# The last attention by query tiles, and the last sequence's end in two halves of tokens

## What is computed

```
scores = q @ k.T / 4 + bias[b, head] (512 x 512, float32), masked keys get -1e30
src    = norm(...) + softmax(scores) @ v @ Wo + bo
out    = src + gelu2((norm(src) * g2 + beta2) @ W1 + b1) @ W2 + b2
```

## Time and profile before

| | before |
|---|---|
| median of 3 runs | 1198.31 us (1197.61 to 1201.12) |
| the profiled execution | 1193.41 us |
| its span, first to last instruction | 1191.5 us |
| PE busy | 987.8 us (83%) |
| PEld, DVE, ACT, POOL busy | 55%, 62%, 58%, 38% |
| mean granted clock of TensorE | 0.961 |

### The profile page before, as it was taken

One profiled execution on the slowest core, in us unless ns is written; L12 is line 12 of the kernel. 1 busy time (PEld: TensorE's weight loads), 2 busy tenths in 40 slices (PEclk: granted clock), 3 DMA queues, 4 the chain that ended last, 5 costly groups with the idle time before them and its releaser, 6 DMA issues.

```text
span 1191.5 us, 22171 instructions
## 1 busy us (share of the span) xinstructions
PE 987.8 (83%) x7620; PEld 653.0 (55%) x7620; DVE 735.1 (62%) x1965; ACT 691.7 (58%) x1603; POOL 447.7 (38%) x672
## 2 busy tenths in 40 slices
PE   5377889898898797888789898799789998689768
PEld 2144555556465365555555576456466575447545
DVE  4368774564837638866773557746874857564750
ACT  1256666473746554676556556675666667366732
POOL 8000020000100636646035003945779436685820
PEclk9589999999899998999999999999899999899989
DMA  7846512405012564575623227557483456944700
GB/s 207 217 122 183 101 37 74 105 1 142 1 37 63 142 160 145 165 196 172 160 86 95 60 89 172 181 161 200 149 217 126 137 170 182 238 146 132 240 1 18
DMA packets 118113, 155.83 MB, mean 131 GB/s; under 512 B 12716, under 2 KB 80684, under 8 KB 118004
## 3 DMA queue, kind: packets, MB, share of 16 engines
q1 hardware_dynamic: 111748, 146.26, 44.5%
q10 hardware_dynamic: 4256, 4.19, 1.4%
q0 software_dynamic: 2000, 3.97, 1.3%
HBM read 135.51 MB, written 18.88 MB: 130 GB/s over the span
## 4 chain that ended last, share of the span: by engine, by line
PE 44%; DVE 20%; ACT 11%; issue 9%; DMA 8%; POOL 5%; SPq 2%; ACTq 0%; DVEq 0%; POOLq 0%
PE bank L1241 14%; PE bank L1230 7%; PE bank L1315 6%; PE bank L1329 4%; POOL bias L739 4%; PE bank L1297 4%; DVE bias L1086 3%; DVE mrow L1080 3%; DMA bias<-in_fside_Bx16xSxS 3%; PE bank L1196 3%; DMA k_parts<-gT 2%; ACT gT L816 2%; SPq L573 2%; DMA ks<-k_parts 2%; ACT bias L768 2%
## 5 line engine op out<-in xcount | busy, mean ns | idle before, releaser
L739 POOL TENSOR_TENSOR bias<-bias,negmask 128x256 f32<-128x256 f32 x512 | 334.5, 684 | 277.3 <-DMA bias<-in_fside_Bx16xSxS 271.5
L768 ACT ACTIVATE bias<-bias,mrow 128x512 f32<-128x512 f32 x256 | 184.2, 720 | 204.2 <-DVE mrow L1086 202.9
L1086 DVE CUSTOM_DVE_ANT_0 bias<-bank,bias 128x512 f32<-128x512 f32 x256 | 175.1, 687 | 189.5 <-PE bank L1297 167.8
L765 ACT ACTIVATE prob<-bank,mrow 128x128 f32<-128x128 f32 (+3 forms) x256 | 135.0, 528 | 198.2 <-DVE mrow L1080 196.8
L1297 PE MATMUL bank<-ks,qs 128*128 128x512 bf16 (+3 forms) x512 | 179.5, 351 | 69.1 <-ACT prob L765 35.5
L1080 DVE TENSOR_REDUCE mrow<-bank 128x1 f32<-128x128 f32 (+3 forms) x256 | 124.4, 487 | 174.6 <-PE bank L1300 173.4
L1315 PE MATMUL bank<-ident,bias 128*128 128x128 f32 x1024 | 161.2, 281 | 55.8 <-ACT pT L776 44.4
L1230 PE MATMUL bank<-hT,w 128*128 128x512 f32 x384 | 184.1, 610 | 11.0 <-ACT gT L816 9.9
L1315 PEld LDWEIGHTS bank<-ident,bias 128*128 128x128 f32 x1024 | 123.2, 144 | 122.7 <-ACT bias L768 70.9
L1241 PE MATMUL bank<-w,gT 128*128 128x256 f32 x768 | 174.3, 381 | 0.0
L1241 PEld LDWEIGHTS bank<-w,gT 128*128 128x128 f32 x768 | 142.5, 190 | 20.2 <-issue 2.7
(11 more groups left out here) (152 smaller groups left out, 1129.8 us busy)
## 6 DMA issues: line engine op xcount, KB each, us to landing
bias<-in_fside_Bx16xSxS SPq DMA_DIRECT2D x128, 512.0 KB, 4.6
w<-in_L_cond_W SPq DMA_DIRECT2D x16, 1024.0 KB, 5.5
qs<-q_parts SPq DMA_DIRECT2D x30, 384.0 KB, 9.7
ks<-k_parts SPq DMA_DIRECT2D x30, 384.0 KB, 11.4
q_parts<-gT SPq DMA_DIRECT2D x80, 128.0 KB
k_parts<-gT SPq DMA_DIRECT2D x48, 128.0 KB
w<-in_L_cond_Wi SPq DMA_DIRECT2D x4, 1024.0 KB, 5.1
w<-in_L_cond_Wo SPq DMA_DIRECT2D x4, 1024.0 KB, 5.5
```

Of the source, the lines that this page charges most:

```text
L739: pool.tensor_tensor(b_n, b_n, negmask[:, t, keys], ALU.add).then_inc(masked, 1)
L765: act.activation(prob_of(U), score_bank[U % 2][:, 0:n], ACT.Exp, bias=mrow[:, U % ROW_RING:U % ROW_RING + 1], accum_out=rsum[:, U % ROW_RI ...
L768: act.activation(prob_of(U), prob_of(U), ACT.Exp, scale=-1.0, bias=mrow[:, U % ROW_RING:U % ROW_RING + 1], accum_out=rsum[:, U % ROW_RING: ...
L1086: v.tensor_tensor_reduce(out=prob_of(U), in0=score_bank[U % 2][:], in1=prob_of(U), scale=-1.0, scalar=3e38, op0=ALU.add, op1=ALU.min, accu ...
```

## The change

In the last attention the query tile is outermost (`unit`): units 448 to 463 are tile 0 with all heads, and so on; a batch is one tile, `values` and `normalize` write accordingly. The second half of the heads is first read in unit 456 and not in 480, and its stack moves from tick 452 to 449. The end of sequence 3 becomes two halves of 256 tokens, each planned by `plan_half`: the first from tick 488, when two tiles are normalized, the second from tick 520. Each half projects, adds, normalizes, turns, does the eight hidden steps and gelus on its 256 columns, its two `ff_out` into bank 1, its addition, and a store from SP's queue. A half does its own two `bn_aggr`; the small rsqrt steps run in full in both. The gelu groups come in ticks 499, 503 and 506. The copies of units 486 to 494 go to ACT by the planner's costs and those of units 495 to 506 to DVE, where before they alternated. POOL's mask terms come in ticks 444, 460, 476 and 492 instead of 444, 452, 460 and 468. ACT's final wait for the stores becomes SP's.

```
+def plan_half(t, s, i):
+    at(t, "pe", "project", s, 1, i)
+    at(t + 1, "v", "residual", s, 1, i)
+    at(t + 2, "v", "stats", s, 6, i)
+    for r in range(RSQRT_STEPS):
+        at(t + 3 + r // SLOTS, f"v{r % SLOTS}", "rsqrt", s, 6, r, i)
+    at(t + 6, "v", "apply", s, 6, i)
+    at(t + 7, "p", "res_l3_half", s, i)
+    at(t + 7, "pe", "turn_half", s, i)
+    at(t + 8, "v", "feature_cols", s, i)
+    at(t + 8, "a", "feature_cols", s, i)
+    t += 10
+    for j, (dt, da) in enumerate(zip((0, 0, 1, 3, 4, 5, 7, 8), (1, 1, 1, 5, 5, 5, 8, 8))):
+        at(t + dt, "pe", "hidden_cols", s, i, j)
+        at(t + da, "a", "gelu_cols", s, i, j)
+    for x in range(2):
+        at(t + 9 + x, "pe", "ff_out", s, 2, 2 * i + x)
+    at(t + 11, "v", "ff_add", s, 2, i)
+    at(t + 12, "sp", "store_half", s, i)
...
-STACKS_AT = [(-6, 5)] + [(-28, 4)] * 2 + [(-7, 4)] + [(-28, 4)] * 3 + [(-7, 4)]
+STACKS_AT = [(-6, 5)] + [(-28, 4)] * 2 + [(-7, 4)] + [(-28, 4)] * 3 + [(-7, 1)]
...
-    [(9, norm(6), 3), (15, block3, 3)],
...
+HALF_AT = [40, 72]
+for _i, _t in enumerate(HALF_AT):
+    plan_half(UNITS * LAST_ATT + _t, LAST_SEQ, _i)
...
             c, t, e, j = u // (2 * NT * GH), u // (2 * GH) % NT, u // GH % 2, u % GH
+            if a == LAST_ATT:
+                t, c = u // (4 * GH), u // (2 * GH) % 2
...
+            def store_half(s, i):
+                sp.wait_ge(ff_done, 2 * FFN[s, 2] + i + 1)
+                tt = slice(2 * i, 2 * i + 2)
+                sp.dma_start(out[s].rearrange("(t p) d -> p t d", p=P)[:, tt, :], xy[s][:, tt, :]).then_inc(stored, 16)
...
+            def res_l3_half(s, i):
+                pool.wait_ge(tok[5], NT * NTH[s, 5] + 2 * (i + 1))
+                for t in (2 * i, 2 * i + 1):
+                    res(pool.tensor_tensor(xy[s][:, t, :], xy[s][:, t, :], b2[1][:], ALU.add))
...
+            def gelu_cols(s, i, j):
+                n, cols = FFN[s, 2], slice(HALF * i, HALF * (i + 1))
+                act.wait_ge(f1_psum, NF * (n + i) + j + 1)
+                act.activation(gT[:, j, cols], dense_bank[FF_BANK[j]][:, cols], ACT.Gelu_apprx_sigmoid,
+                               bias=b1[2][:, j:j + 1]).then_inc(g_done, 1)
...
+            def turn_half(s, i):
+                dense_banks_free(issued)
+                pe.wait_ge(ff_done, 2 * FFN[s, 2] + i)
+                for t in (2 * i, 2 * i + 1):
+                    pe.wait_ge(tok[5], NT * NTH[s, 5] + t + 1)
+                    for c in range(ND):
+                        mm = pe.transpose(dense_bank[c][:, t * P:(t + 1) * P], h[:, t, c * P:(c + 1) * P], ident[:])
...
+            def hidden_cols(s, i, j):
...
+                if j >= 3:
+                    pe.wait_ge(g_done, NF * (n + i) + j - 2)
+                for c in range(ND):
+                    mm = pe.matmul(dense_bank[FF_BANK[j]][:, cols], w1[:, c, j * P:(j + 1) * P], hT[:, c, cols],
+                                   start=c == 0, stop=c == ND - 1)
...
             def project(s, l, i):
-                if i == 0:
+                if ATT[s, l] == LAST_ATT:
+                    dense_banks_free(issued)
+                    pe.wait_ge(ff_done, 2 * FFN[s, 2] + i)
+                    pe.wait_ge(ctx_norm, BATCHES * LAST_ATT + 2 * (i + 1))
+                elif i == 0:
...
             def scores(U):
-                if U % (UNITS // 2) == 0:
+                if a == LAST_ATT and U % UNITS in (0, 2 * GH) or a != LAST_ATT and U % (UNITS // 2) == 0:
                     pe.wait_ge(stack_in[hd // HH], 96 * (a + 1))
```

More of the change, by code:

```diff
@@ L243, in plan_loads @@
 def plan_loads():
-    ffns = sorted((first_tick("pe", "hidden", s, f), s, f) for s in range(B) for f in range(3))
+    ffns = sorted((first_tick("pe", "hidden_cols" if (s, f) == (LAST_SEQ, 2) else "hidden", *((s,) if (s, f) == (LAST_SEQ, 2) else (s, f))), s, f)
+                  for s in range(B) for f in range(3))
     for n, (_, s, f) in enumerate(ffns):
@@ L286 @@
 TURN = order("pe", "turn_tokens", lambda a: a)
+TURN[LAST_SEQ, 5] = len(TURN)
 NTH = {(s, k): sum(1 for x in TURN if x[1] == k and TURN[x] < n) for (s, k), n in TURN.items()}
+NTH[LAST_SEQ, 5] = sum(1 for x in TURN if x[1] == 5) - 1
 FFN = order("pe", "hidden", lambda a: a[:2])
+FFN[LAST_SEQ, 2] = len(FFN)
 QKV = order("pe", "qk", lambda a: a[:2])
@@ L293 @@
               for t0, sf in sorted((t, a[:2]) for t, e, st, a in EVENTS if e == "pe" and st == "hidden" and a[2] == 0)}
+QKV_BEFORE[LAST_SEQ, 2] = len(ATTENTIONS)
 ADAPT = order("pe", "down", lambda a: a[0])
 assert QKV == ATT and OUTP == ATT and all(ADAPT[s] == s for s in range(B))
[L298 removed]
+V_LOAD = {"stats": 8, "rsqrt": 2, "apply": 9, "apply_late": 9, "feature_half": 7, "feature_cols": 4, "rest": 8, "lo": 8, "v": 8, "residual": 14,
           "ff_add": 12, "expert": 3, "up_add": 7}
[L300 removed]
+A_LOAD = {"feature_half": 7, "feature_cols": 4, "hi": 7, "mid": 7, "gelu": 10, "gelu_cols": 8, "down": 20, "expert": 6}
 def copy_sides():
@@ L502, in res_count @@
                                            if e == "p" and st.startswith("res")):
-                total += NT * (2 if step == "res_l0" else 1)
+                total += {"res_l0": 2 * NT, "res_l3_half": NT // 2}.get(step, NT)
                 if step == name and args[0] == s:
+                    return total
+                if step == "res_l3_half" and (s, layer) == (LAST_SEQ, 3) and args[1] == i_half:
                     return total
@@ L613, in _ @@
                     do[step](*args)
+            sp.wait_ge(stored, 16 * (B + 1))
         @block.gpsimd
@@ L793, in feature_half, with feature_cols @@
                                    bias=norm_w[w][:, 2:3]).then_inc(hT_a, 1)
+            def feature_cols(s, i):
+                cols = slice(HALF * i, HALF * (i + 1))
+                act.wait_ge(t_psum, TURN[s, 5] + 1 + i)
+                act.activation(hT[:, 0, cols], dense_bank[0][:, cols], ACT.Identity, scale=norm_w[2][:, 0:1],
+                               bias=norm_w[2][:, 2:3]).then_inc(hT_a, 1)
             def hi(s, l, i):
@@ L939, in _, with rsqrt @@
             chain = [0]
-            def rsqrt(s, k, i):
+            def rsqrt(s, k, i, half=None):
                 var, bits, guess, sq = nwt[:, 0, :], nwt[:, 1, :], rstd[:], nwt[:, 2, :]
@@ L946, in rsqrt @@
                 if i == 0:
-                    for t in range(NT):
+                    tiles = range(NT) if half is None else range(2 * half, 2 * half + 2)
+                    for t in tiles:
                         count[0] += 1
                         ins = v.bn_aggr(mv[:, t, :], stats[:, t, :])
-                        if t < NT - 1:
+                        if t < tiles[-1]:
                             ins.then_inc(vec, 1)
@@ L1218, in project @@
                 mm.then_inc(wo_psum, 1)
-                if i == 1:
+                if i == 1 and ATT[s, l] != LAST_ATT:
                     issued["out"] += 1
@@ L1237, in ff_out @@
                     pe.wait_ge(w2_in, 16 * (n + 1))
+                done = NF * (n + 1) if (s, f) == (LAST_SEQ, 2) and t == 2 else NF * n
                 for j in range(NF):
-                    if t == 0 and j in (0, 6, 7):
-                        pe.wait_ge(g_done, NF * n + max(6, j + 1))
-                    mm = pe.matmul(dense_bank[FF_OUT_BANK[t // 2]][:, (t % 2) * D:(t % 2 + 1) * D],
+                    if (t == 0 or done > NF * n) and j in (0, 6, 7):
+                        pe.wait_ge(g_done, done + max(6, j + 1))
+                    mm = pe.matmul(dense_bank[ff_out_bank(s, f, t // 2)][:, (t % 2) * D:(t % 2 + 1) * D],
                                    gT[:, j, t * P:(t + 1) * P], w2[:, j, :], start=j == 0, stop=j == NF - 1)
@@ L1244, in ff_out @@
                     mm.then_inc(f2_psum, 1)
-                if t == NT - 1:
+                if t == NT - 1 and (s, f) != (LAST_SEQ, 2):
                     issued["ffn"] += 1
```

49 lines of the change are left out of this document (36 added, 13 removed).

## The result

The changed kernel took 1210.01 us (median of 5 runs, 1201.68 to 1210.66) where the kernel before took 1198.31: ratio 1.0072, with a 95% interval of 1.0044 to 1.0100. It is slower; the forecast was 1199.7 with 1191 to 1206, so the result lies outside the range. The ratio and its interval are estimated from all the runs; the plain quotient of the two medians is 1.0098, so the size of the loss is known only as some 0.4 to 1.0%.

A forecast was written before the change was run, and what follows sets the result against it. Bounds: GpSimd's bias masks in the last attention's second half, then a serial 46.0 us tail. Terms 4.8 + 2.3 + 12.9 - 18.6 = +1.4 us on 1193.41 gave 1194.8, as median 1199.7; range 1191 to 1206.

The forecast's parts named there:

- Part 4: Start of the last attention: unit 456 waits for stack 1, landing at 1041, delaying sequence 2's block; cost 4.8 us.
- The reordered bias addresses I cost at nothing: Start of the last attention: reordered bias loads hidden under PE's work up to 1098 or behind the last load; cost nothing.
- If a bias load were late, POOL would pass it on one for one: Start of the last attention: any lateness of a bias load passes through POOL in full; no size given.
- 16.2 after the landing: From stack 1's landing to the turn of sequence 2's block: 4.8, 10.3 and 1.1 us, so the turn begins at 1057.2.
- Part 3: Ticks 488 to 497: POOL is the limit and gets a mask tile of 1.77 us more; cost 2.3 us (1.8 to 5).
- The rival "by VectorE in ticks 488 to 497": Ticks 488 to 497: cost 5 and a late first turn, +4 us in all, 1203.7 us; chance 0.06.
- Part 2: Ticks 498 to 509: half block beside the attention, ScalarE the limit, 28.2 us for 15.1; cost 12.9 us (10.7 to 14.7).
- The rival by the tables: Half block's gelus: each of six table switches holds ScalarE 1.38 us longer than its row, 1208 us; chance 0.02.
- Part 1: Tail after the last ctxn: half the tokens take 27.4 us instead of 46.0; saved 18.6 us (16.8 to 20.2).
- +1.4: Whole kernel: net of the four parts, 4.8 + 2.3 + 12.9 - 18.6 us, giving 1199.7 us.
- The rival "by the late stack": Start of the last attention: unit 456 waits for stack 1 until 1046.4, +5.4 us over the forecast, 1205.1 us; chance 0.22.

The follow-up runs named there:

- experiment 8: Kernel before with only stack 1's loads moved from tick 452 to 449, its order of units kept: 1206.34 us, ratio 1.0048.
- experiment 2: Changed kernel with units ordered by pairs of query tiles, stack 1 first read in unit 464, its loads still in tick 449: 1207.69 us, ratio 1.0092.
- 5: Changed kernel with units ordered by pairs of query tiles and stack 1 back in tick 452: 1201.64 us, ratio 1.0003.
- 4: Changed kernel by pairs of tiles, stack 1 in tick 449, first half's hidden and output layers moved behind the attention, from tick 521: 1198.59 us, ratio 1.0002.
- 6: Changed kernel by pairs of tiles, first half's hidden and output layers behind the attention, stack 1 in tick 452: 1195.47 us, ratio 0.9959.
- experiment 1: Kernel before with only the last attention's query tile outermost and stack 1 in tick 449, the end left whole: 1209.23 us, ratio 1.0108.
- experiment 9: Changed kernel with POOL's mask added to only 2 of each 256 columns for units 456 to 463 and 488 to 503: 1206.54 us, ratio 1.0064.
- experiment 7: As 6, but the first half's projection, addition, norm and turn start in tick 506 instead of 488: 1191.91 us, ratio 0.9922.
- experiment 3: Changed kernel with the first half's eight gelus replaced by copies with a bias, so without their table loads: 1206.41 us, ratio 1.0075.
- experiment 10: Changed kernel with POOL's mask additions in pieces of 512 columns instead of 256: 1220.84 us, ratio 1.0194.

## Why the prediction was wrong

**Part 4, the start (4.8 forecast, 10.7 measured), is the step that failed.** Its first half was right: the landing of stack 1 came within 0.2 us of 1041. Two things were wrong behind it.
- "The reordered bias addresses I cost at nothing: they lie under PE's work up to 1098 or behind the last load." Two bias loads had been put behind six loads of the stack, and I wrote only that they left the stack's path, not that they now stand in its shadow. Alone this costs 4.2 us in the trace (experiment 8), and undoing it gave 4.1 us back from experiment 2 to 5 and 6.7 from 4 to 6. "If a bias load were late, POOL would pass it on one for one" was the right mechanism and stood there without a price.
- "16.2 after the landing" took 21.9. By its three terms: from the landing to unit 457's maximum 5.8 (4.8 forecast), from there to the end of the rsqrt 14.2 (10.3), the first tile and the turn 1.9 (1.1). Most of the error is the middle term. I let VectorE's norm chain run at its speed of before, 0.16 us a step with POOL idle, and struck out the 2.95 us wait for POOL. But POOL's additions, late with their bias load, now ran beside it: one step took 2.96 and three took 0.6. With the mask loads on SP's queue the middle term was 11.5, but the first 6.8; the stage gave 2.4 us back. How much of the remainder is the reader of unit 456 alone I did not separate: order by tiles with the stack in tick 452 was not run.

**Part 3, ticks 488 to 497 (2.3 forecast, 5.5 measured).** I took POOL for the limit, since it was 12.88 us busy in 13.4, and priced what POOL got. The mask term costs at most 0.2 (experiment 1), so POOL had slack there for nearly all of its 1.8. What costs is what I took for covered: PE's projection, 2.0 us behind the scores of unit 488 with all later transposes and scores queued behind it, and VectorE's chain beside POOL. Taking POOL's additions away gave 2.7 of the 5.5 back (experiment 9), and taking the first half's work away gave all of it (experiment 7). How the 5.5 divides between PE's projection and VectorE's chain was not separated further. The rival "by VectorE in ticks 488 to 497", with 0.06, named the second of the two and put this stage at 5.

**Part 2, ticks 498 to 509 (12.9 forecast, 12.8 measured), was right**, and for its reason. The nine hidden ticks took 18.5 us (18.8 forecast) and the two output ticks 9.4 (9.4). Without the table loads (experiment 3) the nine took 15.1, near the 15.9 of PE's work alone, and ticks 502 and 506, in which PE turns units 500 and 504, were each 1.7 shorter; the forecast had waits of 1.3 and 1.6. So PE's own work is the larger part of the cost, and the wait for ScalarE the rest. As in the earlier trace rows, the gelu begins 0.02 us after its table load. The Trainium skill (ScalarE: Activation LUTs, What ACT_TABLE_LOAD costs) adds a drain of 1.38 us to each switch; the trace does not agree, there is no room for it between 1138.57, 1139.87 and 1141.09. The rival by the tables falls.

**Part 1, the tail (saved 18.6 forecast, 17.3 measured).** The projection is 2.1 us and not 1.1: the row of 1.98 was already that of one half, eight passes. The aggregates to the first hidden matmul took 5.0 for 4.6. Half clock came again (0.50 granted from 1177.3 to 1184.1, behind a stretch in which PE idled), and the hidden layer took 9.0, with 8.7 forecast. The store took 2.6 for 3.1.

**The sum.** 5.9 from part 4, 3.2 from part 3 and 1.3 from part 1 make 10.4 on top of +1.4: 11.8. The medians differ by 11.7; that the two agree so closely is luck, for the ratio of 1.0072 makes 8.6 us of it, and the traces of the two kernels differ by 8.1. The rival "by the late stack" had the place (the start) but not the cause: the stack landed when forecast. The trade was a poor one even as forecast: most of the 17.3 us of tail went into 12.8 us in ticks where PE and ScalarE had work of their own, and the start took more than the rest. What pays is a hole: experiments 4, 6 and 7 put the same matmuls where PE idled anyway.

## What to carry to other kernels

When a transfer is moved up in a queue, price both sides: what it delays behind it is a term of the sum, with the reader of each delayed load named. An engine at 96% busy is not the limit if it runs ahead of its readers; look at who waits for it. And small operations of VectorE must be priced at the speed that they have beside a busy GpSimd, from rows in which both work.

## What the runs showed of the hardware

- **VectorE beside GpSimd.** A 128x4 operation of a norm chain took 0.15 to 0.17 us with POOL idle. Beside POOL's additions of 0.65 us some still took that, but many took 0.5 to 0.7, and beside additions of 1.14 us (experiment 10) up to 1.07 in the chain shown. The Trainium skill (SBUF — State Buffer, Who interferes with whom) says that the two share one pair of ports as an exclusive lock, held for a whole instruction; the trace agrees, in that the wait grew with POOL's instruction.
- **A load issued by GpSimd can hold a VectorE operation for 2.9 us.** In the traces of the kernel before, of the changed kernel and of experiments 7 and 9, every single operation of VectorE of 2.7 to 3.3 us began within 0.5 us of such an issue, and ended about when POOL's next four additions had ended (from 400 us on, where the attentions with a bias lie). It was to be seen in the kernel before as well (POOL's and VectorE's timelines):

```profile
739.92 0.59 POOL L721 DMA_DIRECT2D maskraw<-in_mask_Bx1xSxS_bk  x1 [0.29 <-POOL negmask L728]
740.54 3.93 POOL L739 TENSOR_TENSOR bias<-bias,negmask 128x256 f32<-128x256 f32 x6
```
```profile
740.09 3.02 DVE L961 SCALAR_TENSOR_TENSOR nwt<-nwt 128x4 f32<-128x4 f32 x1
```

It does not hold every operation. Those that were held read and write SBUF only (the small rsqrt steps, one addition of two SBUF tiles). Copies, reductions and biased maxima that read a PSUM bank and began in the same 0.59 us took 0.67 to 0.69, as elsewhere. So of the 14 issues after 400 us in each of these four traces, two or three held an operation. Issuing the 16 loads from SP's queue removed all of the long operations, and took the ratio from 1.0072 to 1.0015. In experiment 10, where two additions of 512 columns make what four of 256 made, the held operations lasted 2.55 to 2.74 us, and each ended with the second addition. So they ended with the additions of one pair of units, however many those are. Why not with the first of them is open.
